# An attention layer of 1024 sequences: a loop of 120 steps and a rearranged beginning

## The chip, the core and the metric

One core of one Trainium2 chip. The metric is the device time of one execution in microseconds (us). The kernel before took 4330.0 us, the median of three runs (4324.12, 4333.71, 4330.0).

## The reference

One transformer encoder layer in fp32, with post-normalisation, over 16 x 64 = 1024 independent sequences of 128 tokens and 128 features; 8 heads of 16 features, 512 hidden features.

```
q = (x @ wq + bq), k = (x @ wk + bk), v = (x @ wv + bv)      split in 8 heads of 16
scores = einsum('brkhd,brnhd->brknh', q, k) / 4
attn = softmax(scores, over n)
out = einsum('brknh,brnhd->brkhd', attn, v) @ wo + bo
x1 = layernorm(x + out) * ln1_g + ln1_b
ff = relu(x1 @ w1 + b1) @ w2 + b2
result = layernorm(x1 + ff) * ln2_g + ln2_b
```

## The kernel before

**Tiling.** Four sequences make a group, so there are 256 groups of 512 tokens. A tile has 128 partitions: tokens, or features where the tile is turned. Precision is kept by splitting an fp32 value into two fp32r parts (weights and x, three products each) or into three bf16 parts (queries and keys). The six products of parts that the scores need are made in one go: 12 transfers per group (L252) lay the parts under each other in the tile `stack`, 96 rows deep. Its first 96 partitions hold the parts; three more (rows 96 to 98, `PROD` and up) hold, on the side of the queries (index 0), the three parts of the negated row maximum (L246), and on the side of the keys (index 1) the constant one, so that the second score product subtracts the maximum. `stack` has four slots, for four groups in flight. Its ones are written once, at the beginning: slots 0 and 1 by POOL's memset at L270, slots 2 and 3 by POOL's memset at L357, behind POOL's part of the first group.

**Staging.** The kernel is a software pipeline. Every engine has a function `step(t, r)`, and in step r it works on groups r, r-1, ... r-7, each at another stage: x is turned, split and projected for group r (L568, L420, L325, L645), the parts are split and stacked (L372, L480, L378, L277, L252), scores and row maxima are made for r-1 and r-2, the maximum is turned and loaded, the turned scores, exponentials and the product with v come at r-3 and r-4, the output projection and first normalisation at r-5, the feed-forward part at r-6, the end and the store at r-7. The order of the work in a step is written out by hand, on every engine for itself, and all meet by semaphores alone.

**The loop.** `iterate` (L182) writes out the steps up to 8 (`LEAD`), then a loop over 240 steps, of which each iteration has `UNROLL` = 48 written out, then the 8 steps from 248 on and up to seven more in which the pipeline runs empty. `LAST` is LEAD + (256 - LEAD) // UNROLL * UNROLL. At the end of an iteration each engine jumps back by itself.

**The beginning.** SyncE issues the first x (L209), then the five transfers on which `qk_loaded` counts (L214), eleven constants (L221), and 16 small ones: each head's rows of wo and of the bias of v, in the places where the heads lie (L225, L226), all counted by `consts_loaded`. Behind them stand the first two x_sb and the next x_blocks. POOL fills the identity, `v_ones` (L265), three small constants and the first ones of the stack (L270), and then takes its part in group 0. VectorE waits for `qk_loaded`, splits wq and wk (L471, L473, two each) and does step 0, which turns x (L568); behind step 0 it splits w1 (L619 to L623), makes `bv_wide` (L625) and, after TensorE's products with it (L786, L788), the biases (L628, L629). ScalarE waits for `qk_loaded` and all of POOL's constants, then does step 0; its first activation, the copy of x at L420, has a table load ahead of it. TensorE waits for the identity and the split weights and does step 0, then the products at L786 and L788. Step 1 begins on all engines once `consts_made` has come.

Of the kernel before, what the change touches and what calls it, by code (L numbers as in the profile page):

```python
# [23 lines left out]

# [4 lines left out]
F32 = mybir.dt.float32  # L29
# [3 lines left out]
ACT = mybir.ActivationFunctionType  # L33
AX = mybir.AxisListType

P = 128
H, D = 8, 16
# [4 lines left out]
HU = 4  # L42
VW = 32
BLK = 32
# [5 lines left out]
PROD = len(Q_PARTS) * D  # L50
STACK_DMAS = 2 * len(Q_PARTS)
MAXROWS = 3
UNROLL = 48
LEAD = 8
DMA = 16


def build(nc, x, wq, bq, wk, bk, wv, bv, wo, bo, w1, b1, w2, b2, g1, be1, g2, be2, out):
# [8 lines left out]
    with ExitStack() as ctx:  # L67
        def sb(name, shape, dt=F32):
            return ctx.enter_context(nc.sbuf_tensor(name, shape, dt))

        def sem(name):
            return ctx.enter_context(nc.semaphore(name))
# [4 lines left out]
        wv_sb, wo_sb = sb("wv_sb", [P, P]), sb("wo_sb", [P, P])  # L77
# [7 lines left out]
        pause = sb("pause", [P, 1])  # L85
# [3 lines left out]
        x_blocks = sb("x_blocks", [P, 2, SEQS * P])  # L89
# [28 lines left out]
        stack_ones_set = sem("stack_ones_set")  # L118
# [35 lines left out]
        def live(t, r, lag):  # L154

            return not isinstance(t, int) or 0 <= r - lag < G

        def upto(t, r, lag, per=1, plus=0):


            plus += per * (r - lag)
            if isinstance(t, int):
                return min(plus, per * G) if plus > 0 else None
            return t * per + plus if plus else t * per

        def upto_dma(t, r, lag, before=0, per=DMA):


            plus = per * ((r - lag) // 2 + 1 - before)
            if isinstance(t, int):  # L170
                return plus if plus > 0 else None
            return t * (per // 2) + plus if plus else t * (per // 2)
# [19 lines left out]
        N_QK, N_CONST, N_SET, N_MADE = 5, 11 + 2 * H, 4, 4  # L192
        block = ctx.enter_context(nc.Block())

        @block.sync
        def _(sp):
            def row(v):
                return v.rearrange("(a m) -> a m", a=1).broadcast_to([P, P])

            def col(v):  # L200
                return v.rearrange("(p a) -> p a", a=1)
# [20 lines left out]

            for h in range(H):
                at = (h % HU) * VW + (h // HU) * D
                sp.dma_start(wo_sb[at:at + D], wo[h * D:(h + 1) * D]).then_inc(consts_loaded, DMA)  # L225
                sp.dma_start(bv_col[at:at + D], col(bv[h * D:(h + 1) * D]),  # L226
                             allow_slow_non_contiguous=True).then_inc(consts_loaded, DMA)
# [32 lines left out]
        def _(pool):  # L260
# [4 lines left out]
            pool.memset(v_ones[:], 1.0).then_inc(consts_set, 1)  # L265
# [3 lines left out]
            pool.wait_ge(consts_set, N_SET)  # L269
            pool.memset(stack[PROD:PROD + MAXROWS, 0:2, 1], 1.0).then_inc(stack_ones_set, 1)  # L270

# [82 lines left out]
            pool.wait_ge(stack_ones_set, 1)  # L354
            step(0, 0)
            pool.wait_ge(lo_split, 2)
            pool.memset(stack[PROD:PROD + MAXROWS, 2:4, 1], 1.0).then_inc(stack_ones_set, 1)  # L357
            pool.wait_ge(stack_ones_set, 2)
# [5 lines left out]
        def _(act):  # L364
            act.wait_ge(qk_loaded, N_QK * DMA)
# [92 lines left out]
            act.wait_ge(consts_set, N_SET)  # L458
# [6 lines left out]
        def _(dve):  # L465
            dve.wait_ge(qk_loaded, N_QK * DMA)


# [70 lines left out]
            def step(t, r):  # L539
# [22 lines left out]
                if live(t, r, 0):  # L562
                    dve.wait_ge(blocks_loaded[r % 2], upto_dma(t, r, 0, per=P // BLK * DMA))
                    if (v := upto(t, r, 0)) is not None:
                        dve.wait_ge(v_done, v)
                    if (v := upto(t, r, 0)) is not None:
                        dve.wait_ge(xT_lo, v)
                    dve.transpose(xT_sb[:], x_blocks[:, r % 2]).then_inc(x_turned, 1)  # L568
# [64 lines left out]
        def _(pe):  # L633
# [157 lines left out]
            pe.wait_ge(stack_ones_set, 2)  # L791
            iterate(pe, step, 1, LEAD, LAST, 6)
# [20 lines left out]
```

## Time and profile before

| | |
|---|---|
| median of three runs | 4330.0 us |
| lowest, highest | 4324.12, 4333.71 us |
| profiled execution | 4320.96 us |
| its span, first to last instruction | 4318.9 us |
| busy: TensorE products, weight loads | 4177.6, 3637.0 us |
| busy: VectorE, POOL, ScalarE | 3703.1, 3615.5, 3420.3 us |
| mean granted TensorE clock | 0.992 of full |

The profile is of one execution. Busy time counts instructions that compute; waits, branches and the issue of transfers are left out. PE is TensorE (products), PEld its weight loads, which overlap with products, DVE is VectorE, ACT is ScalarE, SPq is SyncE's queue of transfers. In the chain that ended last each piece is what released the next; "issue" is time in which an engine waited for nothing that the records show. PEclk is the granted TensorE clock, as a share of full speed. L680 is line 680 of the kernel before.

### The profile page before, as it was taken

How to read it: one execution, taken by the hardware profiler on the slowest of the kernel's cores; microseconds unless marked ns; L12 is line 12 of the kernel's file. 1: busy time of each engine (PE TensorE's matmuls, PEld its weight loads, DVE VectorE, ACT ScalarE, POOL GpSimd, SP SyncE). 2: the span in 40 equal slices, each digit the busy share in tenths (PEclk: the TensorE clock that was granted, in tenths of full speed). 3: DMA queues.
4: the chain of work that ended last, by engine and by line, in shares of the span. 5: the costliest groups of instructions: out<-in, count | busy, mean ns of one | idle time of the engine just before them, and what ended most of it. 6: DMA issues, size and time to landing. Idle time of an engine off the chain costs nothing.

```text
span 4318.9 us, 151819 instructions
## 1 busy us (share of the span) xinstructions
PE 4177.6 (97%) x50954; PEld 3637.0 (84%) x50954; DVE 3703.1 (86%) x9739; ACT 3420.3 (79%) x5889; POOL 3615.5 (84%) x4620
## 2 busy tenths in 40 slices
PE   5999999999999999999999999999999999999998
PEld 4888888888888888888888888888888888888886
DVE  6888888888888888888888888888888888888886
ACT  3888887877887887888888878888887887888886
POOL 5888888888888888888888878888888888888887
PEclk8999999999999999999999999999999999999999
DMA  5555555555555555555655555555555555565552
GB/s 128 146 146 146 149 146 148 148 140 145 149 143 150 144 149 146 142 147 150 150 148 148 146 140 149 146 148 147 147 148 139 148 148 148 146 151 146 149 149 58
DMA packets 1294637, 621.93 MB, mean 144 GB/s; under 512 B 636544, under 2 KB 1293696, under 8 KB 1293824
## 3 DMA queue, kind: packets, MB, share of 16 engines
q1 hardware_dynamic: 1293824, 611.80, 56.8%
q8 instruction: 423, 6.93, 0.7%
q14 instruction: 390, 3.19, 0.2%
HBM read 135.40 MB, written 67.11 MB: 47 GB/s over the span
## 4 chain that ended last, share of the span: by engine, by line
PE 39%; SPq 24%; issue 11%; POOL 10%; DVE 8%; DMA 5%; ACT 1%; DVEq 0%; POOLq 0%; ACTq 0%
SPq L252 14%; PE s_ps L680 6%; DMA stack<-parts 5%; PE oT_ps L707 5%; PE sT_ps L694 5%; PE bankC L645 5%; PE bankB L666 4%; SPq L246 4%; PE bankC L666 4%; SPq L209 4%; PE bankB L645 4%; PE bankA L720 3%; PE bankA L770 3%; POOL xT_parts L325 2%; POOL out_sb L336 2%
## 5 line engine op out<-in xcount | busy, mean ns | idle before, releaser
L404 ACT ACTIVATE prob_sb<-sT_ps 128x1024 f32<-128x1024 f32 x1024 | 1049.5, 1025 | 651.3 <-PE sT_ps L694 640.8
L510 DVE TENSOR_REDUCE max_sb<-s_ps 128x8 f32<-128x1024 f32 x1024 | 1214.3, 1186 | 13.3 <-PE s_ps L680 11.2
L277 POOL TENSOR_TENSOR parts<-rest_sb,parts 128x512 bf16<-128x512 f32 x512 | 585.8, 1166 | 251.7 <-ACT parts L378 251.7
L680 PEld LDWEIGHTS s_ps<-stack 96*128 96x128 bf16 x8192 | 463.2, 98 | 346.4 <-issue 290.0
L680 PE MATMUL s_ps<-stack 96*128 96x128 bf16 x8192 | 638.8, 221 | 84.5 <-DMA stack<-parts 55.2
L694 PE MATMUL sT_ps<-stack 99*128 99x128 bf16 x8192 | 628.6, 219 | 1.3 <-ACT prob_sb L404 1.3
L707 PE MATMUL oT_ps<-prob_sb,v_ones 128*32 128x128 f32 x16384 | 553.4, 276 | 3.4 <-ACT prob_sb L404 2.2
L666 PE MATMUL bankB<-w_sb,h_sb 128*128 128x128 f32 x4096 | 525.2, 281 | 2.3 <-ACT h_sb L385 2.3
L707 PEld LDWEIGHTS oT_ps<-prob_sb,v_ones 128*32 128x32 f32 x16384 | 416.1, 109 | 128.6 <-DVE max_parts L608 51.0
L694 PEld LDWEIGHTS sT_ps<-stack 99*128 99x128 bf16 x8192 | 504.0, 98 | 3.0 <-ACT prob_sb L404 1.8
L666 PE MATMUL bankC<-w_sb,h_sb 128*128 128x128 f32 x4096 | 499.2, 275 | 0.0
L645 PE MATMUL bankB<-nT_parts,w_parts 128*128 128x512 f32 x1536 | 485.9, 424 | 4.6 <-DVE nT_parts L589 4.5
L666 PEld LDWEIGHTS bankB<-w_sb,h_sb 128*128 128x128 f32 x4096 | 476.5, 191 | 13.3 <-ACT h_sb L385 3.6
L385 ACT ACTIVATE h_sb<-bankB,b_col 128x512 f32<-128x512 f32 x512 | 349.7, 683 | 168.9 <-PE bankB L645 168.7
L666 PEld LDWEIGHTS bankC<-w_sb,h_sb 128*128 128x128 f32 x4096 | 478.0, 192 | 0.0
L645 PE MATMUL bankC<-nT_parts,w_parts 128*128 128x512 f32 x1536 | 465.1, 410 | 0.0
L393 ACT ACTIVATE m_sb<-y_sb,shift,rs 128x128 f32<-128x128 f32 x1024 | 448.3, 493 | 6.5 <-POOL shift L347 6.5
L428 ACT ACTIVATE n_sb<-z_sb,shift,rs 128x128 f32<-128x128 f32 x1024 | 418.7, 480 | 1.5 <-POOL shift L310 1.5
L488 DVE STREAM_TRANSPOSE ob_sb<-oT_ps 128x512 f32<-128x512 f32 x512 | 350.6, 685 | 38.4 <-PE oT_ps L707 20.5
L385 ACT ACTIVATE h_sb<-bankC,b_col 128x512 f32<-128x512 f32 x512 | 351.6, 687 | 4.7 <-PE bankC L645 1.1
L336 POOL TENSOR_TENSOR out_sb<-mg_sb,be_row 128x512 f32<-128x512 f32 x256 | 331.3, 1294 | 21.7 <-POOL mg_sb L332 3.2
L299 POOL TENSOR_TENSOR x_sb<-x1g_sb,be_row 128x512 f32<-128x512 f32 x256 | 330.5, 1291 | 21.3 <-POOL x1g_sb L295 2.4
(78 smaller groups left out, 8720.8 us busy)
## 6 DMA issues: line engine op xcount, KB each, us to landing
stack<-parts SPq DMA_DIRECT2D x3072, 128.0 KB, 2.4
x_blocks<-in_x SPq DMA_DIRECT2D x1024, 64.0 KB, 2.8
x_sb<-in_x SPq DMA_DIRECT2D x256, 256.0 KB, 3.3
out<-out_sb SPq DMA_DIRECT2D x256, 256.0 KB, 2.4
stack<-max_parts SPq DMA_DIRECT2D x768, 8.0 KB, 2.2
w_sb<-in_L_conv_w SPq DMA_DIRECT2D x2, 256.0 KB, 3.1
be_row<-in_L_conv_ln_b SPq DMA_DIRECT2D x2, 64.0 KB, 5.3
g_row<-in_L_conv_ln_g SPq DMA_DIRECT2D x2, 64.0 KB, 5.6
```

What stands on the lines that cost most here:

```text
L252: sp.dma_start(stack[j:PROD:len(Q_PARTS), r % 4, c].rearrange("d h x -> d (h x)"), parts[:, r % 2, 3 * c + part]).then_inc(stack_loaded[r ...
L277: pool.tensor_tensor(parts[:, r % 2, 3 * c + LO], rest_sb[:, c], parts[:, r % 2, 3 * c + MID], ALU.subtract).then_inc(lo_split, 1)
L385: act.activation(h_sb[:, c], (B, C)[c % 2][:], ACT.Relu, bias=b1_col[:, c:c + 1]).then_inc(h_ready, 1)
L393: ins = act.activation(m_sb[:, s], y_sb[:, s], ACT.Identity, bias=shift2[:, s:s + 1], scale=rs2[:, s:s + 1])
L404: act.activation(prob_sb[:, s % 2], sT_ps[:], ACT.Exp, scale=float(D) ** -0.5).then_inc(exp_done, 1)
L428: ins = act.activation(n_sb[:, s], z_sb[:, s], ACT.Identity, bias=shift1[:, s:s + 1], scale=rs1[:, s:s + 1])
L510: dve.reduce_max(max_sb[:, (r - lag) % 2, :, s], s_ps[:].rearrange("p (h k) -> p h k", h=H), AX.X).then_inc(max_done, 1)
L645: ins = pe.matmul(bank, w[:, a], xs[:, b], start=k == 0, stop=k == 2)
L666: ins = pe.matmul((B, C)[half][:, s * P:(s + 1) * P], h_sb[:, c, tok], w2_sb[:, c], start=c == 0, stop=c == FC - 1)
L680: ins = pe.matmul(s_ps[:, h * P:(h + 1) * P], stack[0:PROD, (r - lag) % 4, 0, h, tok], stack[0:PROD, (r - lag) % 4, 1, h, tok], start=True ...
L694: ins = pe.matmul(sT_ps[:, h * P:(h + 1) * P], stack[:, (r - lag) % 4, 1, h, tok], stack[:, (r - lag) % 4, 0, h, tok], start=True, stop=True)
L707: ins = pe.matmul(oT_ps[j * VW:(j + 1) * VW, (2 * k + f) * P:(2 * k + f + 1) * P], v_ones[:, (r - lag) % 4, 2 * half + k, h], prob_sb[:, k ...
```

## The change

- `UNROLL` is 120 in place of 48. `LAST` stays 248, so the loop covers the same 240 steps, in two iterations in place of five.
- The ones of the stack are filled as pairs: two bf16 ones are the 32 bits of the fp32 number `TWO_ONES`, so a memset has 4096 elements to a partition in place of 8192. Slots 0 and 1 are filled by VectorE as its first instruction, slots 2 and 3 by POOL behind `v_ones`, ahead of step 0. The memset of POOL behind step 0 is gone.
- POOL fills its three small constants ahead of `v_ones`, which has a semaphore of its own now (`v_ones_set`). POOL's step 0 waits for both halves of the ones.
- The 16 transfers of wo and the bias of v are issued by ScalarE, behind a wait for the three small constants and one exponential of a single column (`pause_act`). Only then does ScalarE wait for `qk_loaded` and `v_ones_set`, and do step 0. On SyncE's queue the first x_sb follows right on the row vectors.
- VectorE turns the first x ahead of its wait for `qk_loaded` and of the casts of wq and wk. In step 0 the turn is left out; in all other steps it stands where it stood.
- TensorE waits for `v_ones_set` ahead of step 1.

```diff
--- before.py
+++ after.py
@@ -22,6 +22,7 @@
 
 
 
+import numpy as np
 import concourse.bass as bass
 from concourse import mybir
 from contextlib import ExitStack
@@ -48,9 +49,10 @@
 Q_PARTS = (HI, HI, HI, MID, MID, LO)
 K_PARTS = (HI, MID, LO, HI, MID, HI)
 PROD = len(Q_PARTS) * D
+TWO_ONES = float(np.array([0x3F803F80], np.uint32).view(np.float32)[0])
 STACK_DMAS = 2 * len(Q_PARTS)
 MAXROWS = 3
-UNROLL = 48
+UNROLL = 120
 LEAD = 8
 DMA = 16
 
@@ -82,7 +84,7 @@
         bo_row, b2_row, be1_row, g1_row, g2_row, be2_row = (sb(n, [P, P]) for n in ("bo_row", "b2_row", "be1_row", "g1_row", "g2_row", "be2_row"))
         bv_wide, ident = sb("bv_wide", [P, P]), sb("ident", [P, P])
         minus_half, minus_one, eps_sb = (sb(n, [P, SEQS]) for n in ("minus_half", "minus_one", "eps_sb"))
-        pause = sb("pause", [P, 1])
+        pause, pause_act = sb("pause", [P, 1]), sb("pause_act", [P, 1])
 
         x_sb = sb("x_sb", [P, 2, SEQS, P])
         xb_sb = sb("xb_sb", [P, 4, SEQS, P])
@@ -115,7 +117,7 @@
 
         qk_loaded, qk_made, consts_loaded = sem("qk_loaded"), sem("qk_made"), sem("consts_loaded")
         ident_zero, ident_set, consts_set = sem("ident_zero"), sem("ident_set"), sem("consts_set")
-        stack_ones_set = sem("stack_ones_set")
+        stack_ones_set, v_ones_set = sem("stack_ones_set"), sem("v_ones_set")
         bv_wide_set, w_products_done, consts_made = sem("bv_wide_set"), sem("w_products_done"), sem("consts_made")
         w1g_set, w_hi_set = sem("w1g_set"), sem("w_hi_set")
 
@@ -189,16 +191,16 @@
             for r in range(last, G + lags):
                 step(0, r)
 
-        N_QK, N_CONST, N_SET, N_MADE = 5, 11 + 2 * H, 4, 4
+        N_QK, N_CONST, N_SET, N_MADE = 5, 11 + 2 * H, 3, 4
         block = ctx.enter_context(nc.Block())
+
+        def col(v):
+            return v.rearrange("(p a) -> p a", a=1)
 
         @block.sync
         def _(sp):
             def row(v):
                 return v.rearrange("(a m) -> a m", a=1).broadcast_to([P, P])
-
-            def col(v):
-                return v.rearrange("(p a) -> p a", a=1)
 
             def by_feature(v):
                 return v.rearrange("(h d a) -> d h a", h=H, a=1)
@@ -219,12 +221,6 @@
                              (bo_row[:], row(bo)), (b2_row[:], row(b2)), (be1_row[:], row(be1)),
                              (g1_row[:], row(g1)), (g2_row[:], row(g2)), (be2_row[:], row(be2))):
                 sp.dma_start(dst, src, allow_slow_non_contiguous=True).then_inc(consts_loaded, DMA)
-
-            for h in range(H):
-                at = (h % HU) * VW + (h // HU) * D
-                sp.dma_start(wo_sb[at:at + D], wo[h * D:(h + 1) * D]).then_inc(consts_loaded, DMA)
-                sp.dma_start(bv_col[at:at + D], col(bv[h * D:(h + 1) * D]),
-                             allow_slow_non_contiguous=True).then_inc(consts_loaded, DMA)
 
             sp.dma_start(x_sb[:, 0], x_g[0]).then_inc(x_loaded[0], DMA)
 
@@ -262,12 +258,12 @@
             pool.wait_ge(ident_zero, 1)
             pool.affine_select(out=ident[:], in_=ident[:], compare_op=ALU.not_equal, fill=1.0, base=0,
                                pattern=[[-1, P]], channel_multiplier=1).then_inc(ident_set, 1)
-            pool.memset(v_ones[:], 1.0).then_inc(consts_set, 1)
             pool.memset(minus_half[:], -0.5).then_inc(consts_set, 1)
             pool.memset(minus_one[:], -1.0).then_inc(consts_set, 1)
             pool.memset(eps_sb[:], EPS).then_inc(consts_set, 1)
-            pool.wait_ge(consts_set, N_SET)
-            pool.memset(stack[PROD:PROD + MAXROWS, 0:2, 1], 1.0).then_inc(stack_ones_set, 1)
+            pool.memset(v_ones[:], 1.0).then_inc(v_ones_set, 1)
+            pool.wait_ge(v_ones_set, 1)
+            pool.memset(stack[PROD:PROD + MAXROWS, 2:4, 1].bitcast(F32), TWO_ONES).then_inc(stack_ones_set, 1)
 
             def lo_part(t, r, c):
 
@@ -351,18 +347,23 @@
                     lo_part(t, r, 0)
                     lo_part(t, r, 1)
 
-            pool.wait_ge(stack_ones_set, 1)
+            pool.wait_ge(stack_ones_set, 2)
             step(0, 0)
-            pool.wait_ge(lo_split, 2)
-            pool.memset(stack[PROD:PROD + MAXROWS, 2:4, 1], 1.0).then_inc(stack_ones_set, 1)
-            pool.wait_ge(stack_ones_set, 2)
             pool.wait_ge(consts_loaded, N_CONST * DMA)
             pool.wait_ge(consts_made, N_MADE)
             iterate(pool, step, 1, LEAD, LAST, 7)
 
         @block.scalar
         def _(act):
-            act.wait_ge(qk_loaded, N_QK * DMA)
+            act.wait_ge(consts_set, N_SET)
+            act.activation(pause_act[:], minus_one[:, 0:1], ACT.Exp)
+
+            for h in range(H):
+                at = (h % HU) * VW + (h // HU) * D
+                act.dma_start(wo_sb[at:at + D], wo[h * D:(h + 1) * D]).then_inc(consts_loaded, DMA)
+                act.dma_start(bv_col[at:at + D], col(bv[h * D:(h + 1) * D]),
+                             allow_slow_non_contiguous=True).then_inc(consts_loaded, DMA)
+
 
             def hi_part(t, r, c):
 
@@ -455,7 +456,8 @@
                 if live(t, r, 6):
                     apply2(t, r, 6, 0)
 
-            act.wait_ge(consts_set, N_SET)
+            act.wait_ge(qk_loaded, N_QK * DMA)
+            act.wait_ge(v_ones_set, 1)
             step(0, 0)
             act.wait_ge(consts_loaded, N_CONST * DMA)
             act.wait_ge(consts_made, N_MADE)
@@ -463,9 +465,19 @@
 
         @block.vector
         def _(dve):
+            dve.memset(stack[PROD:PROD + MAXROWS, 0:2, 1].bitcast(F32), TWO_ONES).then_inc(stack_ones_set, 1)
+
+            def turn_x(t, r):
+
+                dve.wait_ge(blocks_loaded[r % 2], upto_dma(t, r, 0, per=P // BLK * DMA))
+                if (v := upto(t, r, 0)) is not None:
+                    dve.wait_ge(v_done, v)
+                if (v := upto(t, r, 0)) is not None:
+                    dve.wait_ge(xT_lo, v)
+                dve.transpose(xT_sb[:], x_blocks[:, r % 2]).then_inc(x_turned, 1)
+
+            turn_x(0, 0)
             dve.wait_ge(qk_loaded, N_QK * DMA)
-
-
             for k, (w_parts, w_in) in enumerate(((wq_parts, wq_in), (wk_parts, wk_in))):
                 w_hi, w_rest = (w_parts[:, part].rearrange("p (d h) -> p h d", h=H) for part in (HI, REST))
                 dve.tensor_copy(w_hi, w_in[:]).then_inc(w_hi_set, 1)
@@ -559,13 +571,8 @@
                     invert(t, r, 0)
 
                 row_max(t, r, 1)
-                if live(t, r, 0):
-                    dve.wait_ge(blocks_loaded[r % 2], upto_dma(t, r, 0, per=P // BLK * DMA))
-                    if (v := upto(t, r, 0)) is not None:
-                        dve.wait_ge(v_done, v)
-                    if (v := upto(t, r, 0)) is not None:
-                        dve.wait_ge(xT_lo, v)
-                    dve.transpose(xT_sb[:], x_blocks[:, r % 2]).then_inc(x_turned, 1)
+                if live(t, r, 0) and (r > 0 or not isinstance(t, int)):
+                    turn_x(t, r)
                 if live(t, r, 6):
                     add_y(t, r, 0)
                     dve.wait_ge(y_done, upto(t, r, 6, per=2, plus=1))
@@ -789,6 +796,7 @@
             ins.then_inc(w_products_done, 1)
             pe.wait_ge(consts_made, N_MADE)
             pe.wait_ge(stack_ones_set, 2)
+            pe.wait_ge(v_ones_set, 1)
             iterate(pe, step, 1, LEAD, LAST, 6)
```

## Rows read from the trace of the kernel before

**Rows 1.** The page: busy us of each engine (share of the span), instructions.
```profile
PE 4177.6 (97%) x50954; PEld 3637.0 (84%) x50954; DVE 3703.1 (86%) x9739; ACT 3420.3 (79%) x5889; POOL 3615.5 (84%) x4620
```

**Rows 2.** The page: the chain that ended last, share of the span by engine.
```profile
PE 39%; SPq 24%; issue 11%; POOL 10%; DVE 8%; DMA 5%; ACT 1%; DVEq 0%; POOLq 0%; ACTq 0%
```

**Rows 3.** Waits: who waited for whom, us in total, times, longest.
```profile
PE s_ps L680 <- issue: 18.5, 4, 4.8
```

**Rows 4.** Windows: stretch, length, busy us (instructions) by engine, PEclk, DMA, GB/s.
```profile
150.00:920.00 770.00, 759.22 (x9318) 662.56 (x9315) 674.07 (x1782) 624.46 (x1078) 658.65 (x845) 1.00 0.59 147
920.00:950.00 30.00, 25.23 (x283) 21.72 (x282) 20.72 (x54) 19.04 (x33) 18.86 (x23) 0.89 0.47 110
...
2510.00:2540.00 30.00, 25.14 (x276) 21.61 (x275) 20.77 (x51) 19.00 (x33) 19.44 (x24) 0.89 0.47 110
...
3305.00:3335.00 30.00, 25.41 (x284) 22.17 (x282) 20.88 (x50) 19.00 (x34) 19.60 (x25) 0.89 0.49 116
...
4100.00:4130.00 30.00, 29.79 (x376) 26.11 (x375) 26.00 (x71) 24.10 (x43) 25.33 (x31) 1.00 0.60 147
```

**Rows 5.** Chain at the first jump back: start us, us, what.
```profile
922.34 4.69 issue
```

**Rows 6.** Timeline of the first 40 us: start us, us, engine, line, operation, [idle before].
```profile
0.74 1.98 SPq L209 DMA_DIRECT2D x_blocks<-in_x  x4
...
1.42 3.51 POOL L265 MEMSET v_ones<- 128x4096 f32 x1
...
5.10 6.92 POOL L270 MEMSET stack<- 3x8192 bf16 x1
...
7.34 4.82 DVE L471 CAST wq_parts<-wq_in 128x128 fp32r<-128x128 f32 x1 [7.34 <-DMA bk_col<-in_L_conv_bk]
...
10.65 0.43 SPq L221 DMA_DIRECT2D be_row<-in_L_conv_ln_b  x1
...
12.50 0.27 DVE L471 CAST wk_parts<-wk_in 128x128 fp32r<-128x128 f32 x1
...
13.92 1.28 ACT L420 ACT_TABLE_LOAD   x1 [13.92 <-DVE xT_sb L568]
...
15.21 0.63 ACT L420 ACTIVATE xT_parts<-xT_sb 128x512 fp32r<-128x512 f32 x1
...
17.40 1.62 PE L645 MATMUL bankA<-xT_parts,wq_parts 128*128 128x512 f32 x3 [17.40 <-POOL xT_parts L325]
...
18.54 0.42 SPq L229 DMA_DIRECT2D x_sb<-in_x  x1
...
21.73 1.33 DVE L619 TENSOR_SCALAR w1g_sb<-w_sb,g_col 128x512 f32<-128x512 f32 x1
...
22.80 7.79 SPq L252 DMA_DIRECT2D stack<-parts  x12
...
24.13 7.09 POOL L357 MEMSET stack<- 3x8192 bf16 x1
...
24.99 6.30 DVE L625 TENSOR_SCALAR bv_wide<-ident,bv_col 128x128 f32<-128x128 f32 x1
...
31.44 0.77 PE L786 MATMUL s_ps<-wo_sb,bv_wide 128*128 128x128 f32 x2 [9.28 <-DVE bv_wide L625]
...
34.02 0.70 DVE L568 STREAM_TRANSPOSE xT_sb<-x_blocks 128x512 f32<-128x512 f32 x1
...
39.82 1.08 PE L680 MATMUL s_ps<-stack 96*128 96x128 bf16 x8
```

**Rows 7.** The page's groups: line, engine, operation | busy us, mean ns | idle before.
```profile
L510 DVE TENSOR_REDUCE max_sb<-s_ps 128x8 f32<-128x1024 f32 x1024 | 1214.3, 1186 | 13.3 <-PE s_ps L680 11.2
```

**Rows 8.** The page's DMA issues: count, KB each, median us to landing.
```profile
x_blocks<-in_x SPq DMA_DIRECT2D x1024, 64.0 KB, 2.8
...
stack<-parts SPq DMA_DIRECT2D x3072, 128.0 KB, 2.4
...
g_row<-in_L_conv_ln_g SPq DMA_DIRECT2D x2, 64.0 KB, 5.6
```

## The prediction

> **What bounds the kernel now.** I read the page first. TensorE is busy for 97% of the span [rows 1], so a step of the steady state is as long as TensorE's own work. The chain that ended last agrees: TensorE holds its largest part, SyncE's queue 24%, and "issue", which is time with no cause in the records, 11% [rows 2]. A change of this kind leaves the work of a step alone, so I looked for time outside the steps.
>
> The list of waits has what the loop costs. TensorE's first score product (L680, the first instruction of a step) waited for "issue" exactly 4 times, 18.5 us together, 4.8 at most [rows 3]. The loop runs over 240 steps, 48 to an iteration: 5 iterations, 4 jumps back. The chain at the first one shows TensorE standing still for 4.69 us after the last product of a step [rows 5].
>
> The table of windows gives the whole price. In a clean stretch 9318 products ran in 770 us, 12.10 per us. In the four windows of 30 us around the jumps there were 283, 279, 276 and 284 (the second of them, from 1718 us, has no row of its own), on average 280.5, which is 23.2 us of normal work: 6.8 us are lost at each jump. The granted clock of those windows is 0.89 against 1.00 in the clean stretch, so the difference between 6.8 and 4.7 is what the lower of the two clock levels (1.2 for 2.4 GHz) cost after the pause. The fifth end of the body (about 4102 us), where the loop is left and nothing jumps, has 376 products in 30 us and a clock of 1.00 [rows 4]. So the price belongs to the jump taken, not to passing the end of the body.
>
> The third view is the timeline of the beginning. Two things stand out. A VectorE cast of 128x128 takes 4.82 us (7.34 to 12.16) while POOL's memset of the stack's ones runs (5.10 to 12.02), and 0.27 us right after it. And the tensor_scalar that makes bv_wide takes 6.30 us (24.99 to 31.29) while POOL's second memset runs (24.13 to 31.22) [rows 6]. Both times VectorE ends some 0.1 us after POOL does, and TensorE waits behind VectorE.
>
> The Trainium skill, "SBUF — State Buffer", Who interferes with whom, says that VectorE and GpSimd share a pair of ports as an exclusive lock, that casts and tensor_scalar can take it, and that whoever starts second stands still. By that rule the trace agrees: 4.82 against 0.27 us.
>
> **The change, part by part.**
>
> *Loop of 120 steps.* The loop still covers 240 steps, since (256 - 8) // 120 x 120 = 240, so the steps ahead of it and behind it are the same. Two iterations, one jump back: three jumps go, 3 x 6.8 = 20.4 us. Below, the stalls alone would give 3 x 4.7 = 14.1, if the rest of the 6.8 were the phase of my windows. Above, measured against the 376 of the window without a jump, a jump costs (376 - 280.5) / 12.10 = 7.9, together 23.7. I take 20.4, as the mean over four windows with the rate of a long stretch has the least of a window's phase in it.
>
> The Trainium skill, "Runtime: NRT & Kernel Launch", Instruction fetch mechanics, says that the fetch runs ahead only in sequence, and that a taken branch to a target outside the window must fetch it first. By that rule the price stays per jump, whatever the body's length.
>
> *First ones (POOL to VectorE, in pairs).* Half of the stack's ones were 3x8192 in 6.92 us on POOL. As pairs there are 4096 elements; POOL's v_ones, also 4096 to a partition, took 3.51 us [rows 6]. The trace has no long memset on VectorE. Its nearest rows are the reduction, 1186 ns for 1024 elements (1.16 ns each, so 4.7 us) [rows 7], above, and POOL's 3.51 us, below. I take 4.7. It begins near 0.4 us and ends near 5.1. VectorE's next work, turning x, needs the four transfers of x, issued until 2.72 us; with 2.8 us to land [rows 6, 8] they are there at 5.5 and turned at 6.2. Even at 6.92 us it would end at 7.3, and the turned x is wanted by ScalarE only near 10.6 (below). Cost nothing.
>
> *Rest of the ones (POOL).* The small constants now come ahead of v_ones, which ends at 5.0 as before; the other half of the ones then takes 3.5 us, to 8.6. The casts become ready at 7.34 as before (last weight landed) and are held until 8.7, not 12.16. From the end of the first cast to the end of the last VectorE subtraction it took 1.04 us (the turn of 0.70 us was over at 13.92, when ScalarE's table load begins, so the casts at 13.2) [rows 6]. The weights are made at 9.7 us, not 13.2.
>
> *ScalarE.* It waits for the three small constants (about 1.6 us), loads its table (1.28 us), does one exponential (about 0.2), and issues 16 transfers. On SyncE those filled 11.1 to 18.54 us, 0.46 us each [rows 6], 7.4 us together. So ScalarE is free at 10.6. It now ends last: x turned at 6.2, weights at 9.7. Its copy of x starts at 10.6 and not at 15.21, of which 1.28 is the table load that is no longer in the way. I take 4.6. The trace has no transfer issued by ScalarE. If one occupies it for nothing, the weights set the pace: the first product at 9.8 instead of 17.40, gain 7.6. If one costs as much as those of the stack, 7.79 / 12 = 0.65 us [rows 6], ScalarE is free at 13.6: gain 1.6. I take 0.46 us, since these are the very transfers, of the same sizes.
>
> *SyncE's queue.* Without the 16 it is 7.4 us further at x_sb. It is then idle until the first group's parts are split, so the 7.4 buy nothing themselves. Nothing is delayed by them: 12 stack transfers start at 22.80 - 4.6 = 18.2, end at 26.0 and land at about 28.5, and the first scores (39.82 before) would be wanted at 39.8 - 10.6 = 29.2 [rows 6, 8]. That is close: 0.7 us is all the cover there is.
>
> *Constants.* The VectorE work on w1 (L619) started at 21.73, behind the first group; it would now start at 17.1. The last row vectors are issued at 10.65 and take 5.6 us to land [rows 6, 8]: 16.3. ScalarE's last is issued at 10.2, and even at those 5.6 us it lands by 15.8. Cover 0.8 us. If the first group gained 7.6, this would be late and leave 21.73 - 16.3 = 5.4.
>
> *Second ones.* POOL's memset of 7.09 us behind the first group is gone. From L619 to L625 nothing changes (3.26 us). L625 then takes 0.3 us (the free cast of the same shape took 0.27) where it took 6.30: 6.0 us. Behind it TensorE's products with w1 and wo start at 31.44 - 4.6 - 6.0 = 20.8, and the second group is turned at 23.4, not 34.02 [rows 6]. What is late next is the second group's own chain, the same as before. From there on the fill of the pipeline moves earlier as a block, by 10.6.
>
> Head: 4.6 + 6.0 = 10.6; at the ends 1.6 + 6.0 = 7.6 and 5.4 + 6.0 = 11.4.
>
> **Sum.** 20.4 + 10.6 = 31.0 us. The profiled execution took 4320.96 us (span 4318.9 and 2.1 around it): 4289.9. The median of the three runs is 4330.0, 9.0 above the profiled execution, so for a median I say 4330.0 - 31.0 = 4299. At the ends of the costs: 14.1 + 7.6 = 21.7, 4308; 23.7 + 11.4 = 35.1, 4295.
>
> **Rivals.**
>
> *The loop gives, the head doesn't.* The transfers on ScalarE and those on SyncE go at the same time and delay each other or the weights, or the 0.7 us of cover at the first stack transfers is gone and SyncE's queue, with 24% of the chain, sets the pace of the fill anyway. For it: the two thin covers above. Against: 6.0 of the 10.6 us come from a memset that is simply absent. Half the head lost: 4299 + 5 = 4304; all of it: 4309.6.
>
> *The head gives, the loop doesn't.* The pause at a jump grows with the body's length, 2.5-fold, so that one jump costs 17 us and the three that go are paid for: 27.2 before, 17 after, a gain of 10.2 only, which gives 4309; with no gain at all 4319.4. For it: TensorE's stall is called "issue", so the records don't name its cause. Against: there is no trace of anything that would read the whole body.
>
> *Slower: the pauses feed the clock.* Four times the engine rests for 4.7 us. If the chip grants 2.4 GHz only because of these rests, a run of 1970 us without one loses clock in its middle. Each drop as at a jump costs 6.8 - 4.7 = 2.1 us; from 15 more drops on the gain of 31 is gone, and with 25 the kernel takes 4299 + 52 = 4351. Against: the clean stretch of 770 us and the window at 4100, almost 800 us behind the last jump, are both at 1.00 [rows 4], so nothing sinks over a whole iteration. For: no row shows a stretch as long as 1970 us without a jump.
>
> *It doesn't do what it says.* The ones on VectorE hold POOL instead (v_ones later by up to 4.7 us). POOL's ones then end at 13.3, the casts at 14.4, which is 1.2 later than before; the head keeps 6.0 - 1.2 = 4.8. Time 4305.
>
> The Trainium skill, "SBUF — State Buffer", Who interferes with whom, says that a VectorE instruction with at most one input in SBUF, outside the two-port modes, does not contend with GpSimd; no row here shows a long VectorE memset.
>
> **How the numbers follow.** Forecast as worked out (4289 to 4312 with the scatter of the runs, 4324.12 to 4333.71, put on the ends): 0.72. Head mostly lost: 0.10. VectorE's ones hold POOL: 0.05. Loop gives little: 0.07. Slower: 0.04, and 0.02 for what I didn't see. A measurement of this kernel can't tell less than about 0.2%, 8.7 us, from no change. All of the first three and half of the fourth are beyond it: faster 0.90, within 0.06, slower 0.04. The range, 4285 to 4315, holds the forecast, both weaker heads and part of the loop's rival.
>
> **What would show it.** Right: one wait of L680 for "issue" of some 4.7 us instead of four; one stretch of lower clock behind the fill, near 2100 us; a clean rate of 12.1 products per us unchanged; the first product at 12.8 and not 17.40; L471 at about 1.3 us and L625 at 0.3; the second turn of x near 23.4. Wrong: a pause at the one jump well above 5 us; a clean rate below 12.0; a granted clock below 1.00 inside an iteration; ScalarE's 16 issues longer than 8 us; L619 waiting for a transfer.

## The result, and the profile after

The changed kernel takes 4296.14 us, the median of 6 runs (4285.12 to 4300.32), the kernel before 4325.24 in 6 runs (4319.13 to 4333.71). The ratio is 0.9927, with a 95% interval of 0.9911 to 0.9943: 31.6 us less, between 25 and 38. The profiled execution took 4296.51 us (before: 4320.96).

The page of the changed kernel, span and busy times [rows 1] and the chain by engine [rows 2]:

```profile
span 4294.7 us, 151567 instructions
...
PE 4172.8 (97%) x50954; PEld 3634.9 (85%) x50954; DVE 3695.1 (86%) x9740; ACT 3419.6 (80%) x5890; POOL 3606.2 (84%) x4619
...
PE 42%; SPq 23%; issue 11%; POOL 10%; DVE 7%; DMA 5%; ACT 1%; DVEq 0%; POOLq 0%; ACTq 0%
```

The work on each engine is what it was, within 0.3%. What shrank is the time between.

The wait of TensorE's first score product (now L687) around the one jump left [rows 3], and windows: clean, around the jump, and where the loop is left [rows 4]:

```profile
PE s_ps L687 <- issue: 3.4, 1, 3.4
```

```profile
150.00:920.00 770.00, 760.23 (x9345) 663.37 (x9344) 674.91 (x1785) 625.89 (x1080) 659.38 (x845) 1.00 0.60 148
...
2090.00:2120.00 30.00, 26.57 (x298) 23.16 (x297) 20.81 (x57) 18.97 (x33) 20.99 (x27) 0.89 0.51 127
...
4100.00:4130.00 30.00, 28.61 (x366) 24.94 (x365) 25.19 (x64) 23.68 (x43) 25.47 (x33) 1.00 0.61 149
```

One pause in place of four, 3.4 us, not 4.7. The clean rate is 9345 / 770 = 12.14 per us. The window of the jump has 298 products, so 30 - 298 / 12.14 = 5.5 us are lost there.

The timeline of the beginning [rows 6]:

```profile
0.73 1.28 ACT L359 ACT_TABLE_LOAD   x1 [0.73 <-PEq L812]
...
1.52 3.51 POOL L264 MEMSET v_ones<- 128x4096 f32 x1
1.63 0.43 ACTq L363 DMA_DIRECT2D wo_sb<-in_L_conv_wo  x1
1.65 3.47 DVE L468 MEMSET stack<- 3x4096 f32 x1 [1.65 <-PEq L812]
...
5.15 0.71 DVE L477 STREAM_TRANSPOSE xT_sb<-x_blocks 128x512 f32<-128x512 f32 x1
...
7.33 1.40 DVE L483 CAST wq_parts<-wq_in 128x128 fp32r<-128x128 f32 x1 [1.47 <-DMA bk_col<-in_L_conv_bk]
...
8.75 0.45 ACTq L364 DMA_DIRECT2D bv_col<-in_L_conv_bv  x1
...
9.33 0.63 ACT L421 ACTIVATE xT_parts<-xT_sb 128x512 fp32r<-128x512 f32 x1 [7.10 <-issue]
...
10.65 0.43 SPq L223 DMA_DIRECT2D be_row<-in_L_conv_ln_b  x1
...
11.52 1.62 PE L652 MATMUL bankA<-xT_parts,wq_parts 128*128 128x512 f32 x3 [11.52 <-POOL xT_parts L321]
...
12.15 7.38 SPq L211 DMA_DIRECT2D x_blocks<-in_x  x4
...
18.50 0.49 DVE L626 TENSOR_SCALAR w1g_sb<-w_sb,g_col 128x512 f32<-128x512 f32 x1 [2.57 <-DMA be_row<-in_L_conv_ln_b]
19.02 0.43 DVE L628 CAST w_parts<-w1g_sb 128x512 fp32r<-128x512 f32 x1
...
19.58 7.79 SPq L248 DMA_DIRECT2D stack<-parts  x12
20.09 0.28 DVE L632 TENSOR_SCALAR bv_wide<-ident,bv_col 128x128 f32<-128x128 f32 x1
...
23.10 0.70 DVE L477 STREAM_TRANSPOSE xT_sb<-x_blocks 128x512 f32<-128x512 f32 x1
...
29.29 1.03 PE L687 MATMUL s_ps<-stack 96*128 96x128 bf16 x8 [0.21 <-DMA stack<-parts]
```

To be seen: VectorE's ones and POOL's v_ones run side by side; v_ones takes the 3.51 us that it took before. VectorE's row has 3.47 us and ends at 5.12. It begins at 1.65, while ScalarE and POOL begin at 0.73, and no row says what VectorE did until then. ScalarE issues its 16 transfers from 1.63 to 9.2 us, 0.47 each. The first product comes at 11.52 (17.40), the second turn of x at 23.10 (34.02). And two things are late that were not before: VectorE waits at L626 until 18.50 for the last row vector (issued at 10.65), and SyncE needs 7.38 us, not some 2, to issue four transfers of x.

### The profile page after: what moved, and what is told of

Its sections match the earlier page's. It is cut to its first block, busy times and chain, and to the rows that moved or that the text cites. A ratio compares the mean times of both kernels' runs of the same rounds, so it can differ in the third digit from the quotient of the medians.

```text
span 4294.7 us, 151567 instructions
## 1 busy us (share of the span) xinstructions
PE 4172.8 (97%) x50954; PEld 3634.9 (85%) x50954; DVE 3695.1 (86%) x9740; ACT 3419.6 (80%) x5890; POOL 3606.2 (84%) x4619
## 4 chain that ended last, share of the span: by engine, by line
PE 42%; SPq 23%; issue 11%; POOL 10%; DVE 7%; DMA 5%; ACT 1%; DVEq 0%; POOLq 0%; ACTq 0%
SPq L248 13%; PE s_ps L687 6%; PE oT_ps L714 6%; PE sT_ps L701 5%; PE bankC L652 5%; DMA stack<-parts 5%; PE bankB L673 5%; PE bankC L673 4%; SPq L242 4%; PE bankB L652 4%; SPq L211 3%; PE bankA L727 3%; PE bankA L777 3%; POOL xT_parts L321 2%; POOL out_sb L332 2%
## 5 line engine op out<-in xcount | busy, mean ns | idle before, releaser
L687 PEld LDWEIGHTS s_ps<-stack 96*128 96x128 bf16 x8192 | 463.2, 98 | 338.3 <-issue 282.0
L687 PE MATMUL s_ps<-stack 96*128 96x128 bf16 x8192 | 638.9, 221 | 77.5 <-DMA stack<-parts 63.4
L500 DVE STREAM_TRANSPOSE ob_sb<-oT_ps 128x512 f32<-128x512 f32 x512 | 349.9, 683 | 26.8 <-PE oT_ps L714 22.4
L332 POOL TENSOR_TENSOR out_sb<-mg_sb,be_row 128x512 f32<-128x512 f32 x256 | 331.7, 1296 | 20.7 <-POOL mg_sb L328 1.3
```

Source lines behind the costliest of these rows:

```text
L687: ins = pe.matmul(s_ps[:, h * P:(h + 1) * P], stack[0:PROD, (r - lag) % 4, 0, h, tok], stack[0:PROD, (r - lag) % 4, 1, h, tok], start=True ...
```

## The experiments

The expectations speak of "step 12". It is the 13th turn of the row maxima (L763, L770 after the change), counted from 0; the pipeline is full by then. The cuts of code are shortened; `...` and words in comments stand for what is left out.

**Jumps.** Four kernels ran beside the kernel before on one chip. The loop alone:

```diff
-UNROLL = 48
+UNROLL = 120
```

> The kernel before with UNROLL = 120 alone; the beginning is untouched. Theory A (each jump back costs about 6.9 us, whatever the body's length): one pause of L680 for issue of about 4.7 us in place of four, 3 x 6.9 = 21 us less than before, about 4304 against 4325, ratio 0.995; the long step at the jump 22 to 24 us. Rival B (the pause grows with the body's length, 2.5-fold): one pause of about 12 us, the step at the jump above 30 us, 10 us less than before, about 4315. In both the second turn of x stays near 34 us.

The new beginning with the old loop:

```diff
 # changed kernel
-UNROLL = 120
+UNROLL = 48
```

> The changed kernel with UNROLL = 48 again: the new beginning alone. Theory A (the beginning's 10 us are partly given back while the pipeline fills, because TensorE has the lower clock there for longer): second turn of x near 23 us, but step 12 only 7 to 8 us earlier than before (245.6), about 4317.5. Rival C (the 10 us stay whole, the rest is scatter of the steps): step 12 at 235 or earlier, about 4314.5. Both: four pauses of about 4.7 us and steps of 23 us as before.

Nine jumps (UNROLL = 24 in the changed kernel):

> The changed kernel with UNROLL = 24: ten iterations, nine jumps back in place of one. Theory A (price per jump, about 6.9 us): 8 x 6.9 = 55 us more than the changed kernel, about 4351, 0.6% slower than before; nine pauses of about 4.7 us. Rival B (pause grows with the body's length): each of the nine pauses about 1 us in place of 4.7, total below 4310.

And none:

```diff
 # changed kernel, in iterate
-            with eng.Fori(first, last - UNROLL + 1, UNROLL) as t:
-                for r in range(UNROLL):
-                    step(t, r)
+            for r in range(first, last):
+                step(0, r)
```

> The changed kernel with no loop at all: all 256 steps written out, no jump and no register in a wait. Theory A: the last jump's 6.4 to 6.9 us go as well, about 4289, and no pause of L680 for issue. Rival D (the program's length costs something in every step, for instance in its fetch): the clean rate falls below 12.1 products per us and the time is above 4296. Rival E (2400 us and more without a pause lower the granted clock): stretches of clock below 1.00 in the middle.

| kernel | jumps | median us | ratio to before (95%) |
|---|---|---|---|
| before | 4 | 4321.37 | |
| loop of 120 alone | 1 | 4304.34 | 0.9957 (0.9943 to 0.9970) |
| new beginning, loop of 48 | 4 | 4320.43 | 0.9995 (0.9986 to 1.0004) |
| new beginning, loop of 24 | 9 | 4351.92 | 1.0078 (1.0064 to 1.0092) |
| new beginning, written out | 0 | 4284.85 | 0.9908 (0.9893 to 0.9924) |

The waits of the first score product for "issue", in us in total, times, longest: loop of 120 alone (around its jump), then loops of 48 and of 24 with the new beginning:

```profile
PE s_ps L680 <- issue: 3.0, 1, 3.0
```

```profile
PE s_ps L687 <- issue: 18.3, 4, 4.8
```

```profile
PE s_ps L687 <- issue: 32.9, 9, 3.9
```

A pause is 3.7 us with a body of 24 steps, 4.6 with 48, 3.0 and (changed kernel) 3.4 with 120. It doesn't grow with the body: rival B falls. With bodies of 24 and 120 it is less than the 4.7 us of the expectations. The total follows the count of jumps: from none to nine the same beginning goes from 4284.85 to 4351.92, 7.5 us a jump. The loop alone gives 0.0043 x 4321 = 18.6 us for three, where 21 was expected.

From one turn of the row maxima to the next, a step with a jump took 23.2 to 23.6 us in the kernel before, 22.4 in the changed kernel, 20.7 with the loop of 120 alone (22 to 24 was expected) and 21.2 to 22.9 with the body of 24; the other steps took 16.4 to 16.5 on average. So 4.3 to 7.2 us are lost at a jump itself. Where the total price of a jump is above that, no run shows where the rest lies.

Written out there is no such pause, and no lower clock in the middle that would matter, so rivals D (the length of the program costs something in each step) and E (the clock sinks without pauses) fall as well:

```profile
250.00:4050.00 3800.00, 3754.57 (x46086) 3274.53 (x46086) 3334.82 (x8803) 3090.28 (x5328) 3258.68 (x4171) 1.00 0.60 147
```

(This is the repeated run of that kernel, below; 3800 us at a clock of 1.00, 46086 / 3800 = 12.13 per us.)

The second kernel missed both theories. Its beginning is as early as it should be, at the 13th turn; kernel before, then new beginning with the loop of 48 (count, duration ns, start us):

```profile
L763 PE MATMUL oT_ps<-ident,max_sb x1: 274/274/274, 245.4 to 245.4; 128*32 128x128 f32 x1
```

```profile
L770 PE MATMUL oT_ps<-ident,max_sb x1: 275/275/275, 235.8 to 235.8; 128*32 128x128 f32 x1
```

9.6 us earlier, and yet its 11 runs are only 2 us faster than before (-6 to +2). Most of its clean stretches are slower than that of the kernel before, 12.05 against 12.10 products per us [rows 4]; two of its windows, and the waits for the stack's transfers of the kernel before and of this one:

```profile
960.00:1700.00 740.00, 725.38 (x8920) 632.65 (x8919) 644.59 (x1698) 596.68 (x1030) 629.69 (x806) 1.00 0.59 147
...
3350.00:4080.00 730.00, 716.68 (x8795) 625.11 (x8799) 636.89 (x1679) 589.29 (x1017) 620.32 (x796) 1.00 0.60 147
```

```profile
PE s_ps L680 <- DMA stack<-parts: 55.2, 91, 3.0
```

```profile
PE s_ps L687 <- DMA stack<-parts: 75.7, 95, 3.3
```

The trace of that kernel is of its slowest run, 4330.00 us against a median of 4320.43, so these rows show more than the median lost: its span is 9.3 us longer than that of the kernel before, while the medians differ by less than 1.

**The parts of the beginning.** Four variants of the changed kernel. The 16 transfers back on SyncE's queue:

```diff
-                act.dma_start(wo_sb[...], wo[...]); act.dma_start(bv_col[...], ...)
+                sp.dma_start(wo_sb[...], wo[...]); sp.dma_start(bv_col[...], ...)   # ahead of x_sb
```

> The changed kernel with the 16 transfers of wo and the bias of v back on SyncE's queue, ahead of the first x_sb. Theory A (ScalarE's issues set the first product, SyncE's queue sets the constants): ScalarE copies x at about 7.5 us and not 9.33, the first product comes at about 10.0 and not 11.52, as the weights are made at 9.8; but the last constant lands near 20.5 and not 18.4, so the work on w1 (L626 of the changed kernel) starts 2 us later and the second turn of x comes at about 25.2, not 23.10. Rival F (the late constant is one of the transfers' bandwidth, not of the queue): with x_sb issued 7.4 us later, the last row vector lands at about 16.3 as before, and the second turn comes at 23 us or earlier. In total within 3 us of the changed kernel, 4293 to 4300, in both.

POOL's ones behind its step 0:

```diff
-            pool.memset(stack[PROD:PROD + MAXROWS, 2:4, 1].bitcast(F32), TWO_ONES)...
-            pool.wait_ge(stack_ones_set, 2)
+            pool.wait_ge(stack_ones_set, 1)
             step(0, 0)
+            pool.wait_ge(lo_split, 2)
+            pool.memset(stack[PROD:PROD + MAXROWS, 2:4, 1].bitcast(F32), TWO_ONES)...
```

> The changed kernel with POOL's half of the ones (still pairs, 3.5 us) behind its step 0, where it stood before. Theory A (a cast or tensor_scalar of VectorE stands still while POOL's memset runs): the first cast takes 0.27 us and not 1.40, and in exchange the first VectorE work on w1, wanted at 18.5, is held until the memset's end near 21.6 us, so the second turn comes near 26 us, not 23.10; the first product stays at 11.5 us, since ScalarE's issues set it. Rival G (the 4.8 and 6.3 us before were not POOL's doing): no VectorE instruction above 0.8 us, second turn at 23.1.

The first x turned in step 0, behind the casts:

```diff
-            turn_x(0, 0)
-                if live(t, r, 0) and (r > 0 or not isinstance(t, int)):
+                if live(t, r, 0):
```

> The changed kernel with the first x turned behind the casts again. Theory A: the turn ends at about 10.5 us, the copy of x comes near 10.5 and not 9.33, the first product near 12.7 and not 11.52; but the last constant lands at 18.4 us whatever the first group does, so the second turn of x moves by less than 0.5 us from 23.10. Rival H (the first group's chain still sets the second turn): it moves by the same 1.2 us.

More work for TensorE where it rests:

```diff
+            for _ in range(32):          # and 12 more at two places
+                pe.transpose(oT_ps[:, 0:P], ident[:], ident[:])
```

> The changed kernel with 32 turns of the identity on TensorE ahead of the first product, 12 ahead of the products with w1 and wo and 12 ahead of step 1, all into a bank that nothing reads: TensorE does more and rests less. Theory A (in the fill TensorE's lower clock is part of the chain): from some point of the first 60 us on the products run at the higher clock (three of 128x512 in about 0.95 us, not 1.62), and step 12 comes 2 to 4 us earlier than 237.9. Rival I (SyncE's queue alone sets the fill): step 12 within 1 us of 237.9, whatever the clock.

| variant | first product | L626 or its like | second turn of x | 13th turn | ratio to before (95%) |
|---|---|---|---|---|---|
| changed kernel | 11.52 | 18.50 | 23.10 | 237.7 | 0.9927 (0.9911 to 0.9943) |
| 16 on SyncE | 10.90 | 19.59 | 24.21 | 237.1 | 0.9939 (0.9923 to 0.9956) |
| POOL's ones late | 11.56 | 17.91 | 25.77 | 237.4 | 0.9952 (0.9934 to 0.9969) |
| x turned late | 12.70 | 17.56 | 23.30 | 237.2 | one run, 4292.95 us |
| TensorE busy | 11.53 | 18.31 | 22.09 | 238.6 | 0.9950 (0.9933 to 0.9966) |

Timeline of the first variant (16 on SyncE), then of the second (POOL's ones late):

```profile
7.33 0.63 ACT L422 ACTIVATE xT_parts<-xT_sb 128x512 fp32r<-128x512 f32 x1 [5.10 <-DMA bk_col<-in_L_conv_bk]
7.33 1.41 DVE L484 CAST wq_parts<-wq_in 128x128 fp32r<-128x128 f32 x1 [1.46 <-DMA bk_col<-in_L_conv_bk]
...
8.68 1.26 POOL L327 TENSOR_TENSOR xT_parts<-xT_sb,xT_parts 128x512 fp32r<-128x512 f32 x1
...
8.77 1.42 DVE L486 TENSOR_TENSOR wq_parts<-wq_in,wq_parts 128x128 fp32r<-128x128 f32 x1
...
10.90 1.62 PE L653 MATMUL bankA<-xT_parts,wq_parts 128*128 128x512 f32 x3 [10.90 <-DVE wk_parts L486]
...
19.56 2.17 SPq L211 DMA_DIRECT2D x_blocks<-in_x  x4
19.59 0.49 DVE L627 TENSOR_SCALAR w1g_sb<-w_sb,g_col 128x512 f32<-128x512 f32 x1 [4.28 <-DMA bv_col<-in_L_conv_bv]
...
21.77 7.75 SPq L254 DMA_DIRECT2D stack<-parts  x12
```

```profile
7.34 0.28 DVE L485 CAST wq_parts<-wq_in 128x128 fp32r<-128x128 f32 x1 [1.48 <-DMA bk_col<-in_L_conv_bk]
...
18.10 3.74 POOL L352 MEMSET stack<- 3x4096 f32 x1
18.43 3.70 DVE L630 CAST w_parts<-w1g_sb 128x512 fp32r<-128x512 f32 x1
```

The transfer engines in the changed kernel, then with the 16 on SyncE (the last two numbers: their busy share, GB/s):

```profile
12.00:16.00 4.00, 3.71 (x12) 2.62 (x11) 1.50 (x2) 1.93 (x4) 0.26 (x1) 1.00 0.84 58
16.00:20.00 4.00, 0.77 (x4) 0.48 (x3) 1.43 (x3) 1.19 (x2) 2.00 (x2) 1.00 0.96 186
```

```profile
12.00:16.00 4.00, 3.72 (x13) 2.68 (x11) 1.50 (x2) 2.52 (x4) 0.88 (x1) 1.00 0.33 81
16.00:20.00 4.00, 0.16 (x1) 0.00 (x0) 0.41 (x1) 0.60 (x1) 1.38 (x2) 1.00 0.09 22
```

*16 on SyncE.* ScalarE's copy moves to 7.33, and the weights, not ScalarE, set the first product; at 10.9, not 10.0, as a VectorE subtraction with two inputs in SBUF (L486, 1.42 us for 0.39) stands still while POOL's subtraction (8.68 to 9.94) runs. The last row vector takes 5.2 us to land, not 7.8 as in the changed kernel, and SyncE's four transfers of x 2.17 us, not 7.38. So both were right in part: the vector is late when x_sb and x_blocks follow at once (rival F), and the transfer engines are then busy for 0.84 and 0.96 of the two stretches above, not 0.33 and 0.09; but with the 16 on SyncE the last of those 16 is later still, and VectorE waits for it until 19.59. In total it is worth nothing measurable to have moved them.

In the changed kernel with TensorE kept busy:

```profile
25.19 0.94 PE L654 MATMUL bankA<-xT_parts,wq_parts 128*128 128x512 f32 x3 [0.75 <-POOL xT_parts L321]
...
30.38 0.62 PE L689 MATMUL s_ps<-stack 96*128 96x128 bf16 x8 [3.54 <-DMA stack<-parts]
```

*POOL's ones late.* The first cast takes 0.28 us, and the second cast for w1 (L630) 3.70 us beside POOL's memset (18.10 to 21.84). The lock is POOL's doing; rival G falls. Second turn 25.77 against the 26 expected. *x turned late.* First product 12.70, second turn 23.30, both as theory A has them. The reason is only in part the late constant: in this execution it came at 17.56, 0.9 us earlier than in the changed kernel, and VectorE waited for it for 0.45 us; then its cast (L627) took 1.26 us and not 0.43, beside POOL, which was later too.

*TensorE busy.* In the second group the products ran at the higher clock level (three in 0.94 us, not 1.62), and the 13th turn came no earlier; its first scores waited 3.5 us for the stack's transfers, whose issue took 9.14 us here and 7.79 in the changed kernel. Theory A's 2 to 4 us didn't come. But the variant raised the granted clock only up to 32 us (0.92 and 0.93 of full in the stretches 24 to 28 and 28 to 32, against 0.50 and 0.72); from 32 to 60 us it was as low as before (0.50 to 0.67). What a higher clock over the whole fill would give is not shown. Nor is it shown that SyncE's queue alone sets the fill (rival I): in the changed kernel's chain from 35 to 240 us the issues of the stack's transfers hold 14.7%.

All variants reach the 13th turn between 237.1 and 238.6 us, though the second turn differs by 3.7. The same beginning reached it at 234.9 to 237.7 in six kernels, so differences below some 3 us can't be told there. This holds for each part of the new beginning: only the beginning as a whole is seen at the 13th turn, not how its gain divides among the parts.

**The beginning without jumps.** As no jump disturbs them, the two beginnings were compared written out; then constants that step 6 needs first were moved behind step 0:

> The kernel before with all 256 steps written out and its beginning untouched: the four jumps alone. Theory A (7 us per jump): 28 to 32 us less than before, ratio about 0.993, step 12 at 246 us as before, and 9 us slower than the changed beginning written out in the same way (next run). Rival J (what the beginning gains by step 12 is lost again in later steps): within 3 us of the next run.

> The changed kernel with all steps written out, once more, beside the kernel before written out. Theory A: step 12 at 236 to 237 us and 9 us less in total than the kernel before written out; 37 to 40 us less than before. Rival J: step 12 the same, the total within 3 us of the kernel before written out.

```diff
 # changed kernel, written out
-  sp:  w1, w2, g1_col, be1_col, b1_col, bo_row, b2_row, be1_row, g1_row, g2_row, be2_row
+  sp:  w1, g1_col, be1_col, b1_col, bo_row, b2_row, be1_row
+  act: (behind its step 0) w2, g1_row, g2_row, be2_row -> late_loaded
+  pool, pe: wait_ge(late_loaded, 4 * DMA) ahead of step 6
```

> All steps written out, and the four constants that no engine needs ahead of step 6 (w2, g1_row, g2_row, be2_row) issued by ScalarE behind its step 0, with a semaphore of their own. Theory A (the last constants land late because all large loads share the transfer engines): the rest of the constants land before 16 us, the work on w1 starts at about 16.0 and not 18.5, the second turn of x at about 22 and not 23.1, and SyncE's next x_blocks no longer take 7 us to issue, so the first stack transfers start at 18.0 and not 19.6; step 12 gains at most 1.6 us, total about 4283. Rival K (the fill has its own pace and swallows it): step 12 the same as in the run before within 1 us.

The last kernel is the changed one with `UNROLL = 60`.

> The changed kernel with UNROLL = 60: four iterations, three jumps. It tells whether the missing gain of the changed beginning at UNROLL = 48 was the beginning's or that program's own. Theory A: 7 us for the one jump less and 9 us for the beginning, about 16 us less than before, ratio 0.9963. Rival J (the beginning's gain is lost in the steps): 7 us less, ratio 0.9984.

| kernel | jumps | median us | ratio to before (95%) | 13th turn |
|---|---|---|---|---|
| before | 4 | 4321.07 | | 245.4 |
| before, written out | 0 | 4289.03 | 0.9922 (0.9908 to 0.9936) | 245.1 |
| changed, written out | 0 | 4277.90 | 0.9901 (0.9886 to 0.9917) | 235.3 |
| the same, four constants late | 0 | 4276.06 | 0.9894 (0.9879 to 0.9909) | 236.0 |
| new beginning, loop of 60 | 3 | 4306.19 | 0.9971 (0.9961 to 0.9980) | 235.7 |

Written out, the new beginning is worth 11.1 us by the medians and 0.0021 x 4321 = 9.1 by the ratios, as much as the 9.8 at the 13th turn. The slowest run with it (4282.06) is faster than the fastest without (4284.20). Rival J falls for these programs. The loop of 60 lies between the theories: 12.5 us (9 to 17) where theory A wanted 16 and rival J 7; its pauses are 3.4 us each:

```profile
PE s_ps L687 <- issue: 10.1, 3, 3.6
```

The kernel with late constants starts L628 at 15.79 and turns the second x at 22.06, as expected. The issue of x_blocks still took 5.34 us, but began earlier, so the stack's transfers start at 16.86, earlier than the 18.0 expected. At the 13th turn nothing is gained (236.0 against 235.3); that is what rival K says, but a gain of 1.6 us is less than what can be told there. Its beginning:

```profile
15.79 1.33 DVE L628 TENSOR_SCALAR w1g_sb<-w_sb,g_col 128x512 f32<-128x512 f32 x1
...
16.86 7.78 SPq L245 DMA_DIRECT2D stack<-parts  x12
...
22.06 0.70 DVE L479 STREAM_TRANSPOSE xT_sb<-x_blocks 128x512 f32<-128x512 f32 x1
```

Both written-out kernels with the new beginning beat the changed one: against the kernel before they save 43 and 46 us (40 in the first series), where it saves 32. Between the two there is no difference that could be measured.

## Why the prediction was right

*Three jumps.* Forecast 20.4 us; the loop alone gave 18.6 (13 to 25). That the price is one per jump and no matter of the body's length was right. The size is less even than I took it: 6.2 us a jump in that kernel, 7.5 between none and nine jumps, 8.4 for the four of the kernel before, with the loop's own instructions for waits on registers (151819 instructions against 142389) gone too. One part of the term was taken too high: the jump that stays has a pause of 3.4 us, not 4.7, and loses 5.5 us in its window, not 6.8. The pause varies from 3.0 to 4.8 us; what it depends on is open.

*First ones.* Forecast 4.7 us, ending at 5.1; the row has 3.47 us, near POOL's pace and my lower end, and ends at 5.12, as it begins at 1.65 and not at 0.4. Hidden as forecast. That they would hold POOL fell: v_ones took its 3.51 us. The rule of the Trainium skill, "SBUF — State Buffer", Who interferes with whom, which was cited against this rival, holds in this trace: 3.51 us beside VectorE's memset as without it.

*POOL's ones and the casts.* Released at 8.73 (8.7), weights made at 9.8 (9.7).

*ScalarE.* Forecast free at 10.6, measured 9.3. The price per transfer was right (0.47 us); the start was not: the table load stands ahead of the wait (0.73 us) and is hidden, and the issues begin at 1.63, ahead of the exponential (2.02). This made the first product 1.3 us earlier than forecast.

*The step that failed* is "Constants", with "SyncE's queue". That the work on w1 would wait for a transfer was named beforehand as a sign of being wrong, and it did wait. I let the last row vector land as before, at 16.3. With x_sb issued right behind it, it took 7.8 us and came at 18.5, and the cover of 0.8 us was gone. In the same stretch the issue of x_blocks took 7.38 us (5.34 with four constants fewer, 2.17 behind the 16), so the stack's transfers began at 19.58, not 18.2, and the first scores waited for them, for 0.21 us, until 29.29 (29.2 was forecast). What saved the sum was that by 18.5 POOL had finished, so that L626 and L628 took 0.49 and 0.43 us and not 1.33 and 1.26. Two errors of 1.4 and 1.7 us cancelled: second turn at 23.10, forecast 23.4. That was luck; the mechanism there was not the one forecast.

*The second memset.* L632 took 0.28 us (6.30): 6.0 us, as forecast.

*Head.* Forecast 10.6, measured 9.1 to 11.1 without jumps. With the loop of 120 it is 31.6 less the 18.6 of the loop alone, 13 us, uncertain by some 9, as the two come from different series. The second turn gained 10.9. At the 13th turn the profiled changed kernel is 7.7 us ahead of the kernel before, the one written out 9.8; the difference between these is within what that turn varies. The split of the head into 4.6 for the first product and 6.0 for the second memset was seen only at the second turn of x, not behind the fill.

*Sum.* 31.0 forecast, 31.6 measured (25 to 38). That the two agree within 0.6 us is luck, given that width. The rival of the clock fell: the 3800 us without a jump are at 1.00.

*Open:* with a loop of 48 the new beginning reaches the 13th turn 9.6 us earlier, and the total shows 2 (-6 to +2). In its one trace, of its slowest run, the steps behind the fill are slower by 0.4%, and the waits for the stack's transfers longer by 20 us. The same beginning keeps its gain written out, so I take this to belong to that program, which no run shows; with the loop of 60 the gain lies between none and all of it. The cause was not found. So the sum of the two terms is borne out for the loop of 120 and without jumps, not for every length of the body.

## What to carry to other kernels

Count the jumps back of a loop, look for waits for "issue" of that count, and compare a window around one with one where the loop is left: this gives the price and where it belongs before anything is changed (here 6.8 us by the windows, and 6.2 to 8.4 by the times). When an engine's share of a beginning is moved away, ask what the queue behind it will issue earlier, and what shares the transfer engines with it: a cover of less than 1 us in a stretch full of loads is none. A saving ahead of a pipeline's fill has to be measured behind the fill: 2.7 us at the start of the first stack transfers left nothing there that could be told from the scatter.

## What the runs showed of the hardware

- A taken jump stops TensorE for 3.0 to 4.8 us, with bodies of 24 to 120 steps, and the end of a body without a jump for nothing.
- VectorE's fp32 memset of 4096 elements on three partitions has a row of 3.47 us, POOL's on 128 partitions one of 3.51, at the same time; POOL's on three partitions took 3.51 too. As bf16, with 8192 elements, POOL's took 6.92.
- A VectorE cast stands still beside POOL's memset (3.70 for 0.43 us); a VectorE subtraction with two inputs in SBUF doesn't (L623 of the kernel before, with POOL's L357 from 24.13 us on [rows 6]), but does beside a POOL subtraction (1.42 for 0.39, 16 on SyncE). The row of the former:

```profile
24.39 0.69 DVE L623 TENSOR_TENSOR w_parts<-w1g_sb,w_parts 128x512 fp32r<-128x512 f32 x1
```

- SyncE's queue needed 7.38 us to issue four transfers of x while the transfer engines were busy for 0.84 to 0.96 of the time, and 2.17 for the same four where 0.09 stood just before.
